# Expert stage: the last seven of 23 row tiles narrowed to 128 rows in plain fp32

## What is computed

```python
logits = jnp.einsum('btd,de->bte', X, Wg) + bg
topv, topi = jax.lax.top_k(logits, S)              # S = 2
w = jax.nn.softmax(topv, axis=-1)
xs = X[:, :, None, :] * w[..., None]
out = X
for e in range(E):                                 # E = 8
    h = jax.nn.silu(jnp.einsum('btsd,dh->btsh', xs, W1[e])) * jnp.einsum('btsd,dh->btsh', xs, W3[e])
    y = jnp.einsum('btsh,hd->btsd', h, W2[e])
    mask = (topi == e)[..., None]
    out = out + jnp.where(mask, y, 0.0).sum(axis=2)
```

## Time and profile before

| | |
|---|---|
| median of 3 runs | 1890.05 us (1887.49 to 1890.36) |
| the profiled execution | 1889.55 us |
| its span from first to last instruction | 1887.7 us |
| TensorE busy | 1762.2 us (93%) |
| VectorE / ScalarE / GpSimd busy | 1213.7 / 1113.1 / 459.5 us |
| granted TensorE clock, mean | 0.983 of full speed |

### The profile page before, as it was taken

The page is one execution under the profiler, slowest core; times in us unless marked ns, Lnnn a source line. Parts: engine busy times, 40 slices in busy tenths (PEclk is TensorE's granted clock), DMA queues, the critical chain, the costliest instruction groups (busy, mean ns, idle before and its releaser), DMA issues. The chain is left out here.

```text
span 1887.7 us, 28143 instructions
## 1 busy us (share of the span) xinstructions
PE 1762.2 (93%) x9516; PEld 1114.1 (59%) x9516; DVE 1213.7 (64%) x2860; ACT 1113.1 (59%) x2332; POOL 459.5 (24%) x434
## 2 busy tenths in 40 slices
PE   5799998898899899999999999999988889999997
PEld 3455554455454444444544464445446889999997
DVE  3867876876877576455456455645764876666664
ACT  2467666666667656555455545554564656766664
POOL 2101111110120010000000002000203677777775
PEclk8899999999999999999999999999999999999999
DMA  3000000010003048000000000100007568667660
GB/s 101 1 23 1 1 23 1 1 29 1 1 1 134 1 155 253 1 23 1 1 1 23 1 1 24 34 1 12 24 13 241 161 194 224 192 194 226 196 196 6
DMA packets 123054, 128.12 MB, mean 68 GB/s; under 512 B 10912, under 2 KB 118304, under 8 KB 122912
## 3 DMA queue, kind: packets, MB, share of 16 engines
q1 hardware_dynamic: 114176, 117.65, 19.9%
q0 software_dynamic: 8160, 8.67, 2.5%
q10 hardware_dynamic: 576, 0.00, 0.0%
HBM read 97.43 MB, written 30.69 MB: 68 GB/s over the span
## 5 line engine op out<-in xcount | busy, mean ns | idle before, releaser
L1155 DVE TENSOR_REDUCE l_tile_max<-psum 128x1 f32<-128x512 f32 x512 | 341.9, 688 | 110.4 <-PE psum L833 108.6
L1003 ACT ACTIVATE l_probs<-psum 128x1024 f32<-128x1024 f32 x256 | 248.2, 1022 | 106.8 <-PE psum L845 103.3
L2578 POOL TENSOR_TENSOR moe_w_lo<-moe_w,moe_w_hi 128x512 fp32r<-128x512 f32 x184 | 260.1, 1414 | 122.3 <-ACT moe_w_hi L2360 120.5
L1911 DVE TENSOR_REDUCE l_row_max<-psum 128x2 f32<-128x1024 f32 x124 | 151.7, 1223 | 205.2 <-PE psum L1566 204.6
L833 PE MATMUL psum<-l_kT,l_qT 128*128 128x512 f32 x512 | 238.1, 472 | 40.1 <-DVE l_tile_max L1155 36.8
L2290 PE MATMUL psum<-moe_xs_hi,moe_w_hi 128*128 128x256 f32 x736 | 212.4, 289 | 2.6 <-DVE moe_xs_lo L2410 2.6
L2290 PE MATMUL psum<-moe_xs_lo,moe_w_hi 128*128 128x256 f32 x736 | 210.1, 286 | 0.0
L2290 PE MATMUL psum<-moe_xs_hi,moe_w_lo 128*128 128x256 f32 x736 | 209.9, 285 | 0.0
L833 PEld LDWEIGHTS psum<-l_kT,l_qT 128*128 128x128 f32 x512 | 98.3, 193 | 131.7 <-DVE l_tile_max L1155 111.0
L1754 ACT ACTIVATE l_probs<-psum,l_neg_max 128x512 f32<-128x512 f32 x248 | 167.2, 674 | 0.0
L845 PE MATMUL psum<-l_qT,l_kT 128*128 128x512 f32 x512 | 161.1, 399 | 1.5 <-ACT l_probs L1003 1.5
(11 more groups left out here) (323 smaller groups left out, 3290.5 us busy)
## 6 DMA issues: line engine op xcount, KB each, us to landing
moe_w<-in_moe_w SPq DMA_DIRECT2D x276, 256.0 KB, 4.6
moe_sorted_x<-l_zeros SPq DMA_DIRECT2D x1, 17680.0 KB, 56.0
moe_xs<-moe_sorted_x SPq DMA_DIRECT2D x23, 272.0 KB
moe_w<-in_ctx SPq DMA_DIRECT2D x8, 512.0 KB, 3.7
moe_w<-in_ctxT SPq DMA_DIRECT2D x4, 1024.0 KB, 5.6
moe_w<-in_wkv SPq DMA_DIRECT2D x2, 2048.0 KB, 15.6
x_resid<-in_x SPq DMA_DIRECT2D x4, 512.0 KB, 10.1
out_x<-x_resid SPq DMA_DIRECT2D x4, 512.0 KB
```

The lines of the kernel that those rows point to most:

```text
L1003: nc.scalar.activation(probs[:, n % PT_RING], wide(2 * (n % 2)), ACT.Exp, scale=SCALE).then_inc(exp_done, 1)
L1155: nc.vector.reduce_max(tile_max[:, q % 2, t, h, half:half + 1], bank(max_bank(m)), AX_X).then_inc(max_read, 1)
L1911: nc.vector.reduce_max(row_max[:, t, :], wide(2 * (t % 2)).rearrange("p (j m) -> p j m", j=2), AX_X)
L2578: nc.gpsimd.tensor_tensor(w13_lo[:, k % SPLITS], w13[:, slot_k, :, cols], w13_hi[:, k % SPLITS].bitcast(F32), ALU.subtract).then_inc(w13_s ...
```

## The change

`Shapes` now plans the 18 late tiles as items of units of 128 rows: `BIG` = 11 tiles of 256 rows (pairs of units) and then `SMALL` = 7 tiles of 128 rows (singles). With the first five there are again 23 tiles and 184 steps; tiles 0 to 15 are as before and tiles 16 to 22 (steps 128 to 183) are small (`small[i]`, `is_one(k)`). Each expert's number of units is counted; its pairs are listed first and the single left over, if there is one, in the second list; pairs beyond 11 are listed as two singles.

A small tile isn't split in parts: `up_one` multiplies the raw weights `w13` in the ring's slot with `xs_one` (128 columns), `down_one` the hidden values `hid_one` with the raw `w2`, in plain fp32. In these steps ScalarE and GpSimd round and split nothing and VectorE makes only the product and, once per tile, a copy of the transposed rows. The slot stays in use until TensorE has read it.

```diff
-        self.TILES = TOP * self.T * P // ROWS + self.E - 1
+        units = (TOP * self.T * P - self.FIRST * ROWS + self.E * (P - 1)) // P
+        self.SMALL = self.E - 1
+        self.BIG = -(-(units - self.SMALL) // 2)
+        self.MIXED = self.BIG + self.SMALL
+        self.TILES = self.FIRST + self.MIXED
...
+                    for table, step, half in ((router.pair_no, 1, 0), (router.pair_first, ROWS, P)):
+                        nc.gpsimd.iota(table[:, 0:s.BIG], pattern=[[step, s.BIG]], base=0, channel_multiplier=0,
...
@@ SyncE
-                    sp.wait_ge(w13_split, PIECE * (m - W_SLOTS + 1))
-                    sp.wait_ge(w2_split, PIECE * (m - W_SLOTS + 1))
+                    spent = PIECE * (m - W_SLOTS + 1)
+                    if not is_one(spent - 1):
+                        sp.wait_ge(w13_split, n_full(spent))
+                        sp.wait_ge(w2_split, n_full(spent))
+                    else:
+                        sp.wait_ge(up_psum, spent)
+                        if spent % FT == 0:
+                            sp.wait_ge(y_psum, spent // FT)
+                        else:
+                            sp.wait_ge(one_down, n_ones_down(spent))
...
@@ TensorE
+                def up_one(k):
+                    i, f = divmod(k, FT)
+                    slot_k, cols, _ = arrived(k)
+                    pe.wait_ge(w_ready[slot_k], 48 * (k // PIECE // W_SLOTS + 1))
+                    hid_done(k - 3)
                     for n in range(2):
                         for c in range(s.DC):
+                            last = nc.tensor.matmul(up_bank(k)[:, n * P:(n + 1) * P], w13[:, slot_k, n * s.DC + c, cols],
+                                                    xs_one[:, i % 2, c, :], start=(c == 0), stop=(c == s.DC - 1))
+                    last.then_inc(up_psum, 1)
+                def down_one(k):
+                    i, f = divmod(k, FT)
+                    slot_k, _, row = arrived(k)
+                    hid_done(k)
+                    if f == 0:
+                        pe.wait_ge(y_ready, i - 1)
+                    last = nc.tensor.matmul(y_bank(i)[:, 0:D], hid_one[:, k % 3, :], w2[:, slot_k, row, :],
+                                            start=(f == 0), stop=(f == FT - 1))
+                    last.then_inc(y_psum if f == FT - 1 else one_down, 1)
...
@@ VectorE
+                        if is_one(k):
+                            nc.vector.tensor_tensor(hid_one[:, k % 3, :], up_bank(k)[:, P:2 * P], gate[:, k % 3, 0:P],
+                                                    ALU.mult).then_inc(one_ready, 1)
...
+                    if k == 19:
+                        router.count_units(dve, T)
                     if k == 20:
-                        router.count_tiles(dve, T, 0)
-                        join_tables()
+                        router.skip_units(dve)
+                    if k == 21:
+                        router.sum_units(dve)
                     if k == 22:
-                        router.sum_tiles(dve)
-                        router.list_experts(dve, FIRST, TILES - FIRST)
+                        router.number_items(dve)
+                        router.list_pairs(dve)
                     if k == 23:
-                        router.list_starts(dve, FIRST, TILES - FIRST)
-                        add_first_used()
-                        router.end_starts(FIRST, TILES - FIRST).then_inc(tiles_ready, 1)
+                        router.list_singles(dve)
+                        router.choose_items(dve).then_inc(tiles_ready, 1)
...
@@ GpSimd
-                    if f in (4, 6) and i >= 1:
+                    if f in (4, 6) and i >= 1 and f // 2 - 2 < halves(i - 1):
                         store_results(i - 1, f // 2 - 2)
...
-                for h in range(HALVES):
+                for h in range(halves(TILES - 1)):
                     store_results(TILES - 1, h)
```

More of the change, by code:

```diff
@@ L2217, in y_bank, with halves, is_one, n_full @@
             return bank(i % 2)
+        small = s.small
+        def halves(i):
+            return 1 if small[i] else HALVES
         def tile_stored(queue, i):
-            queue.wait_ge(y_stored[i % 2], 16 * HALVES * (i // 2 + 1))
+            queue.wait_ge(y_stored[i % 2], 16 * sum(halves(j) for j in range(i % 2, i + 1, 2)))
+        def is_one(k):
+            return small[k // FT]
+        def n_full(k):
+            return sum(not is_one(j) for j in range(k))
+        def n_ones(k):
+            return sum(is_one(j) for j in range(k))
+        def n_ones_down(k):
+            return sum(is_one(j) and j % FT < FT - 1 for j in range(k))
         PIECES = STEPS // PIECE
```

215 lines of the change are left out of this document (165 added, 50 removed).

## The result

| | before | after |
|---|---|---|
| median | 1888.77 us (4 runs, 1885.23 to 1890.36) | 1837.57 us (4 runs, 1835.94 to 1840.42) |
| the profiled execution | 1889.55 us, span 1887.7 | 1837.15 us, span 1835.4 |

The ratio is 0.973, 95% interval 0.9709 to 0.975.

The account below looks back on a forecast made before the run. TensorE was taken as the bound from 1550 us on, VectorE during the last batch's routing. 1889.55 - 44.8 (small tiles) + 5.7 (tables) - 2.2 (tail) = 1848.3 us, range 1840 to 1857.

Parts of the forecast that it names:

- What bounds the kernel: TensorE from 1550 us on, 0.120 us per matmul; VectorE while the last batch is routed beside the first tiles.
- The small tiles, -44.8: Last seven tiles: 11.38 us each in plain fp32 against 17.78, 6.40 us less per tile.
- The low end of 0.108: Small tiles' 128-column matmuls: load and stream overlap perfectly, 0.108 us each, making the seven-tile gain -50.2 us.
- The tables, +5.7: Routing tables in steps 19 to 23: 42 VectorE instructions take 9.87 us where 17 took 4.20.
- up to half is absorbed: Lower bound for the tables: added instructions run beside GpSimd's hold-ups, so they cost only +2.8 us.
- The high end: Upper bound for the tables: half-clock stretches after TensorE's idle times, and held-up added instructions, make them cost +11 us.
- The tail, -2.2: After the last matmul: VectorE's scaling falls from 0.75 to about 0.42 us and one store issue is gone.
- The chain behind a step: Small steps: Silu and product, about 1.1 us or less, stay hidden before the down matmul two 1.38 us steps later.
- The weights: Small tiles need 300 GB/s, no wait forecast; the rival that they become the bound: +15 us, 1863, chance 0.07.
- rival 2: Small tiles: TensorE idles repeatedly and gets the half clock, 21.0 us per tile, 1915 us in all; chance 0.04.
- rival 3: Small tiles: load and stream of 128-column matmuls do not overlap, 0.214 us each, 1890 us, no change; chance 0.05.
- Rival 4: Routing tables stall TensorE twice as hard, +11 us, 1854 us in all; chance 0.10.

Follow-up runs that it names:

- light GpSimd: Kernel before, with GpSimd's subtraction cut to 4 of 128 columns in steps 18 to 34: 1876.55 us, ratio 0.9937.
- plain tiles 2 and 3: Changed kernel with tiles 2 and 3 (steps 16 to 31) also in plain fp32, all 256 rows: 1827.60 us, ratio to before 0.9673.
- new_tables_all_full: Changed kernel with its new tables but no small tile, all late tiles full in split form: 1889.30 us, ratio to before 0.9998.
- the three kernels with the new tables: The changed kernel (1837.57 us), the same kernel run again (1836.66 us), and new_tables_all_full.
- small_weights_late: Changed kernel with SyncE waiting ten more steps before refilling a weight slot in the small tiles: 1881.61 us, ratio to before 0.9961.

## Why the prediction was off, point by point

**What bounds the kernel.** Right on both stages. TensorE set the pace from 1550 us on; VectorE, held up by GpSimd, did for most of steps 18 to 34, as the light GpSimd (-12.5) and the plain tiles 2 and 3 (-9.1) show; it also waited 4.5 us for ScalarE's results there, which the prediction didn't look for.

**The small tiles, -44.8.** The mechanism was right, and the step that failed is the choice of 0.120 us because of "the same balance of the two", load and stream. A 128-column pass has 0.111: 64 x 0.009 = 0.6 us per tile, 10.82 in place of 11.38, and seven times this, with a full tile at 17.80 and not 17.78, is 4.1 us. The low end of 0.108 that stood beside it was nearer. The down pairs at 0.43 and the transposes at 0.12 were exact. The 512-column rows above could have told it: the loss shows there too, where the load is no limit, so it goes with a long fp32r stream and not with the balance. By the 107 ns of a weight load, which the prediction takes from the Trainium skill, "TensorE: Matmul & The Clock Gate", section "LDWEIGHTS (loading the stationary operand)", the seven tiles would have come out 1.8 us too low where the sum was 4 too high.

**The tables, +5.7.** The largest error: 5.7 us forecast, -0.4 in the trace of after (-0.8 in new_tables_all_full). Their own price was right. What failed is the sentence "nothing hides it" and the bound below it, "up to half is absorbed". The prediction had the row that explains it, 2.16 us for a 0.41 us instruction, but took the hold-ups as a fixed part of VectorE's load, to which the tables add. They are a wait for GpSimd, and a wait shrinks when other work is put ahead of it. It also took VectorE to be working or held up all the time, from a slice of 5 us, while 4.5 us of steps 18 to 34 were a wait for ScalarE's results. In the runs the hold-ups shrank by 2 us net and this wait by some 4. Half was a guess and not a bound: hold-ups and waits together were some 19 us (14.3 + 4.5), so a bound from below had to be no cost at all.

**The clock beside the tables.** The high end assumed that longer idle times give more stretches at the half clock. It didn't fall: the mean over steps 18 to 34 is 0.93 before and 0.93 to 0.96 in the three kernels with the new tables.

**The tail, -2.2.** 2.65 measured; the 0.64 us that TensorE waited before its last matmuls, now gone, was not priced.

**The chain behind a step** never showed, as forecast: 0.2 us of waiting for `hid_one` in 56 steps.

**The rivals.** The weights came in time (303 GB/s on average where 300 was the need, with slices up to 376), and small_weights_late shows that the lead is what secures it. The clock was 1.00 from 1750 to 1800 us, so rival 2 never arose. Load and stream overlap, so rival 3 falls. Rival 4 had the sign of the tables' error wrong.

**The range.** 1840 was the low end with 0.108 per pass and half of the tables absorbed. With 0.108 and all of them absorbed it would have been 1837.2 and held the time, though by 0.4 us only; with 0.111 it would have been 1838.5. The forecast erred in two terms by 4 and 6 us, both the same way. The range failed in the second one, whose lower bound was drawn in the middle of what was possible.

## What to carry to other kernels

Ask of every long instruction on a bounding engine whether it works or waits. Added work ahead of a wait for another engine can be free up to the length of the wait; price it between nothing and its full cost, and look at what its operands need. And where an engine other than TensorE bounds a stretch, a form that costs TensorE more and the others less can be the faster one: here 0.43 us more matmul per step took 0.5 to 0.6 us off the step.

## What the runs showed of the hardware

- VectorE's `w2_lo`, 256 columns from two operands in SBUF, takes 0.41 us alone and 0.97 on average beside GpSimd's subtractions (2.16 the longest shown); one on 8 columns took 1.23 in place of 0.17. Instructions with a single operand in SBUF were held up as well: L605 on 8 columns 1.02 us in place of 0.17, the scaling of 256 columns 0.80 on average in place of 0.35. Cutting GpSimd's subtraction to 4 of 128 columns in 17 steps gave 12.5 us.
- Matmuls with a load each: 0.111 us apart at 128 columns (plain passes), 0.112 (split), 0.120 at 256 columns in the split form, 0.23 at 512 columns in fp32r, and 0.216 for a plain pass of 256 columns (1.73 us for eight).
- Repeated waits of TensorE of up to 3.6 us in small_weights_late left a granted clock of 0.86 to 0.94.
- The DMA engines brought up to 376 GB/s in a slice of 2.3 us and 349 in one of 7.5 us, nearly all of it 256 KB transfers from SyncE's queue.
